# A two-layer decoder on one core: coupling's twist by GpSimd copies, and output products ordered by head pairs

## What is computed

```python
def _twist(x):
    o_r, o_i, p_r, p_i = jnp.split(x, 4, axis=-1)
    return jnp.concatenate([p_r, -p_i, -o_r, o_i], axis=-1)
gf = _global_net(x.mean(axis=1, keepdims=True), ...)
out = x
for _ in range(3):
    tf = _coupling_net(out, ...)          # four layers, gelu, gelu, gelu, sigmoid
    combined = 0.7 * gf + 0.3 * tf
    coupling = 0.1 + adaptive_range * (combined - 0.5) * 2.0
    out = out + coupling * _twist(out)
return out                                # residual sum and layer norm follow
```

## Time and profile before

| | us |
|---|---|
| median of 3 runs | 1091.97 (1090.35 to 1094.4) |
| the profiled execution | 1094.54 |
| its span | 1092.8 |
| PE busy | 992.6 (91%) |
| DVE busy | 729.5 (67%) |
| ACT busy | 703.5 (64%) |
| POOL busy | 570.8 (52%) |
| mean granted clock of PE, share of full speed | 0.963 |

### The profile page before, as it was taken

How to read it: one execution, slowest core, us unless ns; L and a number is a source line. 1 busy time by engine, 2 the same in 40 slices (tenths; PEclk the granted TensorE clock), 3 DMA queues, 4 the chain that set the end, 5 groups by cost and what they waited for, 6 DMA issues and landing times.

```text
span 1092.8 us, 16271 instructions
## 1 busy us (share of the span) xinstructions
PE 992.6 (91%) x5218; PEld 780.5 (71%) x5218; DVE 729.5 (67%) x1589; ACT 703.5 (64%) x1397; POOL 570.8 (52%) x437
## 2 busy tenths in 40 slices
PE   6959889999998469999899999999999999998895
PEld 3737678888887257777778788888788887876332
DVE  6876876556566557778686776757776758761257
ACT  4346544333334337888786888868888868886453
POOL 8111310045717306777675877757777757785001
PEclk9989999999999569999999999999999999998898
DMA  7100000000001022223131132213132313210001
GB/s 240 8 1 1 1 1 1 1 1 1 1 1 39 20 64 68 58 56 70 43 82 44 44 83 59 68 42 82 45 83 52 76 42 77 49 43 1 0 0 40
DMA packets 46399, 46.14 MB, mean 42 GB/s; under 512 B 23095, under 2 KB 29163, under 8 KB 45803
## 3 DMA queue, kind: packets, MB, share of 16 engines
q1 hardware_dynamic: 46315, 45.10, 17.2%
HBM read 7.60 MB, written 1.05 MB: 8 GB/s over the span
## 4 chain that ended last, share of the span: by engine, by line
PE 79%; DVE 9%; ACT 5%; issue 4%; POOL 1%; DMA 1%; SPq 0%; POOLq 0%; DVEq 0%; ACTq 0%
PE PS L1592 76%; PE PS L1604 2%; DVE X_ODD L1107 1%; DVE BIG L1190 1%; DVE mx L1187 1%; DVE mxm L1453 1%; ACT BIG L787 1%; DVE st L1089 1%; ACT PHI L1039 1%; DVE X_EVEN L1107 1%; POOL PLO L745 1%; ACT BIG L817 1%; POOL rs L650 1%; DVE mv L1095 0%; DMA QB<-TQ 0%
## 5 line engine op out<-in xcount | busy, mean ns | idle before, releaser
L745 POOL TENSOR_TENSOR PLO<-BIG,PHI 128x512 fp32r<-128x512 f32 (+1 forms) x320 | 413.1, 1291 | 186.4 <-ACT PHI L1039 174.4
L1038 ACT ACTIVATE BIG<-PS 128x512 f32<-128x512 f32 (+1 forms) x320 | 192.4, 601 | 99.9 <-PE PS L1592 94.0
L1453 DVE TENSOR_REDUCE mxm<-PS 128x1 f32<-128x512 f32 x256 | 174.4, 687 | 63.6 <-PE PS L1592 60.2
L1039 ACT ACTIVATE PHI<-PS 128x512 fp32r<-128x512 f32 (+1 forms) x320 | 191.2, 597 | 0.0
L1592 PE MATMUL PS<-KA,QA 128*128 128x512 f32 (+1 forms) x512 | 139.4, 338 | 7.8 <-issue 7.4
L650 POOL TENSOR_TENSOR rs<-ve,half_neg 128x4 f32<-128x4 f32 (+1 forms) x29 | 30.3, 1046 | 220.1 <-DVE ve L1097 219.4
L1592 PE MATMUL PS<-QA,KA 128*128 128x512 f32 (+1 forms) x320 | 129.9, 406 | 6.4 <-issue 6.0
L1592 PE MATMUL PS<-PHI,VLO 128*128 128x512 f32 (+1 forms) x320 | 131.4, 411 | 0.0
L1592 PE MATMUL PS<-PLO,VHI 128*128 128x512 f32 (+1 forms) x320 | 126.4, 395 | 1.0 <-POOL PLO L745 1.0
L1592 PE MATMUL PS<-QB,KB 128*128 128x512 f32 (+1 forms) x320 | 126.1, 394 | 0.0
L1592 PE MATMUL PS<-PHI,VHI 128*128 128x512 f32 (+1 forms) x320 | 125.9, 393 | 0.0
(11 more groups left out here) (264 smaller groups left out, 1984.2 us busy)
## 6 DMA issues: line engine op xcount, KB each, us to landing
KA<-TK SPq DMA_DIRECT2D x128, 128.0 KB, 2.4
QA<-TQ SPq DMA_DIRECT2D x64, 128.0 KB, 2.3
QB<-TQ SPq DMA_DIRECT2D x64, 128.0 KB, 2.3
KA<-TK SPq DMA_DIRECT2D x128, 19.5 KB, 1.8
X_EVEN<-in_x SPq DMA_DIRECT2D x4, 256.0 KB, 3.6
VXA<-in_L_ffn_Wg SPq DMA_DIRECT2D x1, 1024.0 KB, 5.7
VXA<-in_L_ffn_Wu SPq DMA_DIRECT2D x1, 1024.0 KB, 7.6
VXA<-in_L_ffn_Wd SPq DMA_DIRECT2D x1, 1024.0 KB, 9.2
```

The source lines that it names most:

```text
L745: pool.tensor_tensor(PLO[0:rows, g % 4, :], PX[0:rows, g % 4, :], PHI[0:rows, g % 4, :].bitcast(F32), ALU.subtract).then_inc(rest_pool, 1)
L1038: act.activation(PX[0:rows, g % 4, :], PS[0:rows, g % 2, :], ACT.Exp, scale=SCALE_W)
L1039: act.activation(PHI[0:rows, g % 4, :], PS[0:rows, g % 2, :], ACT.Exp, scale=SCALE_W).then_inc(lead_ready, 1)
L1453: dve.tensor_reduce(mxm[:, p % 2, h, m:m + 1], PS[:, 2 + g % 2, :], AX.X, ALU.max).then_inc(mu_free, 1)
```

## The change

- `twist` and its product are gone. POOL copies the rows 64 to 127 of `FS[:, b, :]` to rows 0 to 63 of a new tile `SH`, and rows 0 to 63 to rows 64 to 127, two copies for each batch and cycle, one after the other (`turn_halves`). The signs are one value for each partition, +1, -1, -1, +1 by quarters of 32 rows (`sign`), and are multiplied into the coefficients `cA` and `cB`.
- DVE's second instruction of a unit multiplies with `SH` in SBUF, not with the PSUM bank, and waits for the copies (`turned_ready`).
- POOL's copies of the first cycle wait for the last `rstd` of the norm "E", those of later cycles for `state_ready`.
- The output product goes over pairs outside and token tiles inside; it starts once seven pairs' quotients are there, and waits for the last pair's ahead of its last four products.
- For batch 3 the product stands ahead of `input_f`, not behind it.
- The constants: one memset of `sign` in place of that of `twist`, and two short memsets in place of four selects.

```diff
--- before.py
+++ after.py
@@ -180,7 +180,6 @@
         for b in range(B):
             if c == CYCLES - 1 and b == 2:
                 t += [("back", 0), ("back", 1)]
-            t += [("twist", c, b)]
     t += [("back", b) for b in range(B - 2, B)]
     return {key: n for n, key in enumerate(t)}
 
@@ -330,7 +329,7 @@
         hmask_s = sb("hmask_s", [P, NH])
         hm4 = sb("hm4", [P, HPG])
         iota = sb("iota", [P, E])
-        twist = sb("twist", [P, P])
+        sign = sb("sign", [P, 1])
 
         ctx_sb = sb("ctx_sb", [CK, B, D])
         wq0s, wk0s, wv0s, wo0s = (sb(n, [P, P]) for n in ("wq0s", "wk0s", "wv0s", "wo0s"))
@@ -449,6 +448,7 @@
         H3 = BIG[:, 4096:6144].rearrange("p (b n) -> p b n", b=B)
         TH = REG[:, 0:2048].rearrange("p (b n) -> p b n", b=B)
         CP = REG[:, 2048:4096].rearrange("p (b n) -> p b n", b=B)
+        SH = REG[:, 4096:6144].rearrange("p (b n) -> p b n", b=B)
 
         PS = es.enter_context(nc.psum_tensor("PS", [P, 8, 512], F32))
 
@@ -484,7 +484,7 @@
         shift_ready, sum_ready = sem("shift_ready"), sem("sum_ready")
         vhi_ready, lead_ready, rest_pool, rest_dve = (sem(n) for n in ("vhi_ready", "lead_ready", "rest_pool", "rest_dve"))
         q_in, k_in, kt_in = ([sem(f"{n}{r}") for r in range(3)] for n in ("q_in", "k_in", "kt_in"))
-        gs_ready, coef_ready, state_ready, out_sem = (sem(n) for n in ("gs_ready", "coef_ready", "state_ready", "out_sem"))
+        gs_ready, coef_ready, turned_ready, state_ready, out_sem = (sem(n) for n in ("gs_ready", "coef_ready", "turned_ready", "state_ready", "out_sem"))
 
         block = es.enter_context(nc.Block())
 
@@ -494,7 +494,7 @@
         WIDE = ([(wq1s[:, 512 * n:512 * n + 512], WQHI[:, 512 * n:512 * n + 512], WQLO[:, 512 * n:512 * n + 512]) for n in range(2)]
                 + [(MEDT[:], MEDHI[:], MEDLO[:])]
                 + [(wkv1s[:, 512 * n:512 * n + 512], WKVHI[:, 512 * n:512 * n + 512], WKVLO[:, 512 * n:512 * n + 512]) for n in range(4)])
-        N_CONST = 20
+        N_CONST = 18
         N_VBD = 16 * len(value_pieces())
         N_POOL = 23
         N_E_OPERANDS = 21
@@ -609,7 +609,7 @@
             for w in (cn2, cn3, cn4):
                 pool.memset(w[:], 0.0).then_inc(consts, 1)
             pool.memset(hmask[:], 1.0).then_inc(consts, 1)
-            pool.memset(twist[:], 0.0).then_inc(consts, 1)
+            pool.memset(sign[:], 1.0).then_inc(consts, 1)
             pool.memset(v0x[:], 1.0).then_inc(consts, 1)
             pool.memset(wrT[:], 0.0).then_inc(consts, 1)
             pool.iota(topi[:, 0, 0, :], pattern=[[1, E]], base=0, channel_multiplier=0).then_inc(consts, 1)
@@ -623,10 +623,10 @@
             pool.affine_select(out=hmask[:], in_=hmask[:], compare_op=ALU.is_ge, fill=0.0, base=DH - 1,
                                pattern=[[DH, NH]], channel_multiplier=-1).then_inc(consts, 1)
 
-            for n, (fill, off) in enumerate(((1.0, -64), (-1.0, -64), (-1.0, 64), (1.0, 64))):
-                cols = twist[:, 32 * n:32 * n + 32]
-                pool.affine_select(out=cols, in_=cols, compare_op=ALU.not_equal, fill=fill, base=off - 32 * n,
-                                   pattern=[[-1, 32]], channel_multiplier=1).then_inc(consts, 1)
+            for n, lo in enumerate((32, 64)):
+                pool.wait_ge(consts, 16 + n)
+                pool.memset(sign[lo:lo + 32, :], -1.0).then_inc(consts, 1)
+            pool.wait_ge(consts, 18)
             pool.memset(VBD[:], 0.0).then_inc(vbd_zero, 1)
             setup = [0]
 
@@ -771,6 +771,25 @@
                         pool.wait_ge(latlo_ready, LATENT_SPLIT[p] + 1)
             last_layers()
             rstd(("E", B - 1))
+
+            def turn_halves(c, b):
+
+                if c:
+                    pool.wait_ge(state_ready, B * (c - 1) + b + 1)
+                else:
+                    pool.wait_ge(a_free, LA["xT", "F", b] + 1)
+                n = 2 * (B * c + b)
+                pool.wait_ge(rstd_ready, LN["E", B - 1] + 1)
+                if n:
+                    pool.wait_ge(turned_ready, n)
+                pool.tensor_copy(SH[0:DW, b, :], FS[DW:P, b, :]).then_inc(turned_ready, 1)
+                pool.wait_ge(turned_ready, n + 1)
+                pool.tensor_copy(SH[DW:P, b, :], FS[0:DW, b, :]).then_inc(turned_ready, 1)
+
+            for c in range(CYCLES):
+                for b in range(B):
+                    turn_halves(c, b)
+            pool.wait_ge(turned_ready, 2 * B * CYCLES)
             for b in range(B):
                 rstd(("F", b))
 
@@ -1533,7 +1552,7 @@
 
             dve.wait_ge(cn_in, N_CN)
             dve.tensor_scalar_mul(cbias[:, 0:1], cnb[:, 3:4], 0.5)
-            dve.tensor_scalar_mul(cA[:], ar1[:], 0.3)
+            dve.tensor_scalar(cA[:], ar1[:], sign[:], 0.3, ALU.mult, ALU.mult)
             dve.tensor_scalar_mul(cbias[:, 1:2], gnb[:, 2:3], 0.5).then_inc(coef_ready, 1)
             task(EPILOGUE[0])
             dve.wait_ge(pj_free, PJ["yE", B - 1] + 1)
@@ -1548,6 +1567,7 @@
             dve.wait_ge(a_free, LA["gn", 2] + 1)
             link(dve.tensor_scalar(cB[:], gth[:], ar1[:], 0.7, ALU.mult, ALU.mult))
             link(dve.tensor_scalar_add(cB[:], cB[:], 0.1))
+            link(dve.tensor_scalar_mul(cB[:], cB[:], sign[:]))
             def back(b):
                 n = LV["back", b]
                 dve.wait_ge(v_full, n + 1)
@@ -1564,10 +1584,8 @@
                         back(1)
                     dve.wait_ge(a_free, LA["cn", c, 3, b] + 1)
                     link(dve.tensor_scalar(CP[:, b, :], TH[:, b, :], cA[:], cB[:, b:b + 1], ALU.mult, ALU.add))
-                    n = LV["twist", c, b]
-                    dve.wait_ge(v_full, n + 1)
-                    dve.tensor_tensor(CP[:, b, :], CP[:, b, :], bank_v(n), ALU.mult).then_inc(v_free, 1)
-                    dve.wait_ge(v_free, n + 1)
+                    dve.wait_ge(turned_ready, 2 * (B * c + b + 1))
+                    link(dve.tensor_tensor(CP[:, b, :], CP[:, b, :], SH[:, b, :], ALU.mult))
                     dve.tensor_tensor(FS[:, b, :], FS[:, b, :], CP[:, b, :], ALU.add).then_inc(state_ready, 1)
             for b in range(B - 2, B):
                 back(b)
@@ -1965,10 +1983,13 @@
                     ins = pe.transpose(bank[0:2 * NT, P:2 * P], mxt[:, p % 2].rearrange("p h t -> p (h t)"), ident[:])
                 else:
                     b = key[1]
-                    pe.wait_ge(on_ready, 2 * NHP * (b + 1))
-                    for t in range(NT):
-                        for c in range(NHP):
-                            ins = mm(bank[:, P * t:P * t + P], OT[:, c, P * t:P * t + P], wout1s[:, c, :], start=c == 0, stop=c == NHP - 1)
+                    pe.wait_ge(on_ready, 2 * NHP * (b + 1) - 2)
+                    for c in range(NHP):
+                        if c == NHP - 1:
+                            pe.wait_ge(on_ready, 2 * NHP * (b + 1))
+                        for t in range(NT):
+                            ins = mm(bank[:, P * t:P * t + P], OT[:, c, P * t:P * t + P], wout1s[:, c, :],
+                                     start=c == 0 and t == 0, stop=c == NHP - 1, skip_group_check=True)
                 ins.then_inc(pj_full, 1)
 
             for key in PROLOGUE:
@@ -1998,10 +2019,9 @@
                 pe.wait_ge(x_ready, LN["E", b] + 1)
                 lane_a(("xT", "F", b), transposes(tiles_of(xtile("E", b))))
 
-            pe.wait_ge(on_ready, 2 * PAIRS)
+            task(EPILOGUE[0])
             for b in range(B - 1):
                 input_f(b)
-            task(EPILOGUE[0])
             pe.wait_ge(cn_in, N_CN)
             pe.wait_ge(setup_done, N_POOL)
             global_layers = ((gn1, gsum, 64), (gn2, gact1, 32), (gn3, gact2, P))
@@ -2026,8 +2046,6 @@
                     if layer:
                         pe.wait_ge(a_free, LA["cn", c, layer - 1, b] + 1)
                     lane_a(("cn", c, layer, b), lambda bank: mm(bank, w[:], src[:, b, :]))
-                    if layer == 3:
-                        lane_v(("twist", c, b), lambda bank: mm(bank, twist[:], FS[:, b, :]))
                 if c == 0 and layer < 3:
                     gw, gsrc, rows = global_layers[layer]
                     if layer == 0:
```

## The result

| | before | after |
|---|---|---|
| median, first comparison | 1093.07 us (4 runs, 1090.35 to 1094.4) | 1085.65 us (4 runs, 1084.34 to 1087.1) |
| ratio, with its 95% interval | | 0.9936 [0.9909, 0.9963] |
| median, repeated on one chip | 1090.48 us (31 runs) | 1086.98 us (12 runs) |
| ratio | | 0.9952 [0.9931, 0.9973] |
| profiled execution, its span | 1094.54, 1092.8 us | 1086.76, 1084.6 us |

The first comparison says 0.64% faster and the repetition 0.48%, so the gain lies at the edge of what a measurement of this kernel can tell. The repetition has more runs of both kernels, and I go by it: 3.5 us between the medians, 5.2 by the ratio.

The account below looks back on a forecast made before the run. PE is 79% of the chain, the tail from 1000 us read by itself; -7.4 + 1.8 - 0.1 + 2.7 + 2.7 - 1.4 = -1.7, 1092.8 us for the profiled execution; forecast median 1091.6, range 1083 to 1098.

Parts of the forecast that it names:

- rival 1: DVE beside POOL's copies: two-input instructions pass freely, applies scarcely held; -9.9 us, 1082 to 1084.6; chance 0.22.
- (a): Batch 3's output product: starts before the last quotients, ahead of the transposes, at full clock; -7.4 us.
- (b): Coupling without twist products on PE: gains 0.1 us into the second cycle, 2.0 into the third, 2.4 at most at the end.
- (c): POOL's copies of 64 x 512: 0.7 us each, between 0.3 and 1.29, done in time at either end.
- the losing rival: DVE's units of cycles 1 and 2: copies as slow as two-input work, 1.29 us; +8.5 us, 1100; chance 0.15.
- (d): DVE beside POOL's copies: mutual hold; applies +1.8 us, into cycle 2 +2.7, later gain 1.4 rather than 2.4.
- The first bullet: Last applies of norm E on DVE: a copy falls between each two of four; +1.8 us, from 0 to +4.
- (e): Cycle 2's first layer: PE waits for DVE and its clock falls, slowing layer 2; +2.7 us, from 0 to +4.
- rival 3: Cycle 2: copies hold DVE up, but PE's clock isn't lost; -4.4 us, 1087.6 to 1090; chance 0.14.
- The clock at the norm: PE's clock around the norm after the product: it fell before as well, so no difference.
- The starting point: Whole kernel: the profiled execution, 1094.54 us, was taken to stand 2.57 above the median of 1091.97.

Follow-up runs that it names:

- the copies put off: The changed kernel with POOL's copies delayed until norm E's applies or a cycle's four states are done: 1084.96 us, 0.9939 of the kernel before.
- the copies alone: The changed kernel with output product and transposes back in the old order, only the twist by POOL copies left: 1092.97 us, 1.002 of the kernel before.

## Why the prediction was right or wrong

The range, 1083 to 1098, held the result. The forecast of 1091.6, no change that shows, was 4.6 to 6 us too high, and the result lies at the border between "within 0.5%" (0.57) and "faster" (0.26). That the range held it is owed to its width: for the profiled pair the sum was -1.7, and the tail gave -9.6. The nearest sum is rival 1's -9.9, but by luck, since its mechanism, no hold of DVE, is not what the runs show.

- **(a) The product.** Right in mechanism and place: 64 instructions in one block at full clock, and the run with all quotients waited for shows that the early start is 4.0 us of it (11.17 to 7.15), most of the 4.9 that stay when the 1.5 us behind the product are taken off the 6.4. Mis-sized: I took 0.098 us for an instruction by counting records in 2 us, where partly covered ones count too; at full clock one starts every 0.112 us, 64 took 7.3 us, not 6.3, and the stage gave -6.6, not -7.4.
- **(b) The twist.** 0.1 us into the second cycle is what the copies put off show within a tenth: 18.46 to 18.65. Into the third, 12.77 to 10.70 is the 2.0 that I had, without copies beside. At the end 0.6 where I had 0.4.
- **(c) The copies.** 0.7 predicted, 0.61 measured. Whatever it costs that rows change halves is within that 0.61, no more than a fill of the same size (0.63); the losing rival, at 1.29, is out.
- **(d) The hold.** The assumption that a two-input add started behind POOL waits is shown: 0.98 for 0.69. So rival 1 is out. Its price was too high: 0.29 for each instruction, 0.58 a unit and not 0.9. The stage gave +1.54 where (b) and (d) together had +2.6, into the third cycle and on -2.1 and not -1.4. The first bullet is the step that failed: the four applies were held, 2.26 and not 1.12 us, but +1.8 on the path was wrong. I had seen that PE and ACT come 1 us behind DVE and added the hold on top. They cover it, and the stage is 9.43 with or without it. (With the old order, in the copies alone, the hold does lie on the path, with 1.14 us.) What the stage does pay, 1.5 us at equal clock, is the move of the transposes, which I had called covered in (a).
- **(e) The clock in the second cycle.** +2.7 predicted; 0 in the profile of the result, +1.9 in the repetition. Of the five profiles with copies beside units of 2.49 us or more it fell in two. That was rival 3's case in the first profile. My "it falls here too" was too sure. (The 1061.13 in its working stands in no row, has 1061.19; the 0.98 us for a product that it gave is right all the same, 3.92 for four.)
- **The clock at the norm.** "No difference" was wrong for this pair of profiles: the profile before lost 3.9 us to it (9.36 and 13.99 for 7.95 and 11.51), the one after nothing, the largest single error. In the median it is less, since the kernel before doesn't lose it each time.
- **The starting point.** I set the profiled execution against 1091.97, the median shown. More runs put before at 1090.0 to 1090.9 on three chips, and the profiled one stands 3.7 to 4.6 us above.

Sum of the parts against the profile of before: -6.6 (product) + 1.5 (transposes behind it) - 3.9 (clock at the norm) + 1.5 (second cycle) - 2.1 (third) = -9.6, where I had -1.7. I had 0.8 too much gain in (a), and too much loss of 0.3 at the norm, of 3.9 for its clock, of 3.8 in the second cycle and of 0.7 in the third.

## What to carry to other kernels

An order that lets a long reduction begin before its last input is there is worth the wait it fills, and where the wait is long enough to cost PE its clock, that as well. Work handed to GpSimd is not free for a VectorE that reads two operands from SBUF beside it, and here a tensor_scalar with one was held as well: put it where VectorE adds from PSUM, takes statistics or waits, which here made more of the same change than the change itself. Before a toll is put on the path, look at which engine arrives last there: a hold of 1.1 us cost nothing at the norm in the new order and its full size in the old one, and one of 0.3 us cost its full size in coupling's units.

## What the runs showed of the hardware

The spread of equal runs goes with PE's clock. The 35 runs of the kernel before on one chip, by the mean granted clock of the whole execution:

```
clock   runs   us
0.970     5    1088.28 to 1089.31
0.969     5    1088.52 to 1089.69
0.968     1    1090.70
0.967     8    1090.28 to 1091.15
0.966     8    1090.76 to 1091.95
0.965     3    1092.55 to 1092.98
0.963     2    1093.57, 1094.36
0.961     2    1094.72, 1095.32
0.960     1    1097.06
```

One thousandth of mean clock goes with some 0.8 us, so a comparison of medians here is in part one of how often the clock fell. On the chip of the repetition, at 0.966 to 0.967, the changed kernel ran 1084.8 to 1087.1 us (7 of its 12 runs, mean 1086.4) against 1090.3 to 1091.4 (6 of 31 runs, mean 1090.8): 4.4 us at the same mean clock.

How much a GpSimd copy of 64 x 512 (0.61 us when nothing holds it) holds VectorE was new to me too: not by its whole length. A multiply that starts with 0.44 us of the copy still to run (1032.40, the copy ends at 1032.84) grows by 0.29 us, and the copy itself grows to 0.87 or 0.95. A fill holds a tensor_scalar by 0.40 us and a two-input add not at all.
